# A three-layer kernel on one core: turns written out in line, memory weights on POOL, and a new table of marks for every engine

## The chip, the cores and the metric

The kernel runs on one core of a Trainium2 chip. The metric is device time in microseconds for one launch, as the median of several executions. The core has five instruction streams that run side by side, each in its own order: PE (TensorE, matrix products; the profile lists its weight loads apart, as PEld), DVE (VectorE), ACT (ScalarE), POOL (GpSimd) and SP (SyncE, which issues transfers). They meet only at semaphores.

## The reference, cut to what matters

The input x has 16 sequences of 512 rows and 256 columns. Each sequence goes through four blocks, all residual, each after a layer norm:

```python
x = x + attn_a(layernorm(x))   # 16 heads of 16, elu+1 features, 4 memories, causal sums
x = x + ffn(layernorm(x))      # 256 -> 1024 -> 256, ternary weights
x = x + attn_b(layernorm(x))   # 16 heads, rope, causal softmax over 512 keys
x = x + ffn(layernorm(x))      # the same ffn again
# in attn_a, per sequence and head (m is the memory):
rel = einsum('bhsd,mhd->mbhs', sq, memory_norms)
out_m = einsum('bhsd,mhde->mbhse', sq, memories) / clip(rel, EPS, None)[..., None]
weights = softmax(rel.mean(axis=-1), axis=0)          # over the 4 memories
mem_out = einsum('mbhse,mbh->bhse', out_m, weights)
out = g * mem_out + (1.0 - g) * local                 # g = sigmoid(gate)
```

Sequences don't depend on each other.

## The kernel before, in words

**Lanes and turns.** A sequence passes four lanes, one per block: lane 1 (attn_a, buffer xa), F1 (the first ffn, xf), lane 2 (attn_b, xb), F2 (the second ffn, xg). They form a pipeline over sequences. A turn is one step of it: while lane 2 works on sequence t, F2 finishes t-1 and F1 works on t+1; lane 1 ends t+1 and starts t+2. Its second part, `lane1_end`, comes first in a turn and `lane1_start` later. A filling part, one turn without F2 (t = 0), thirteen full turns, and an emptying part make up the run. The thirteen full turns (t = 1 to 13) are the body of a hardware loop, `with pe.Fori(1, B - 2) as it`, on each of the five engines; what is ahead of it and behind it is written out. In the body, semaphore targets such as `due(L, name, it, n)` are expressions of the loop's register; in what is written out they are constants.

**What sets the order.** Each engine's stream is merged from generators, one per lane, which yield a mark ahead of each piece of work; `in_order` always continues the generator with the lowest mark. The marks stand in the table `MARKS`, by lane, engine and kind of piece, with one number for each repetition. They order the instructions of an engine against each other and have no other effect. Kinds that matter here: lane 1 has T (norm), TT, PA (projections), V (values), SK, RM (mean of rel), ST (states), N and NC and NL (causal tiles), WO (output projection); lane 2 has T, PB, V, N (score tiles of head n for the row maxima), NM, NS (score tiles for the exponentials), PV, TP, OT, WO; an ffn lane has FT (norm), XB (adding b2), FTT, UP (eight blocks of the first product), DN (two blocks of the second).

```python
def in_order(*parts):
    heads = [next(part) for part in parts]
    while any(mark is not None for mark in heads):
        n = min((mark, n) for n, mark in enumerate(heads) if mark is not None)[1]
        heads[n] = next(parts[n], None)
```

**Who hands over to whom.** The turn's last DVE piece of F1 is the sum at L1084 that writes `xb`, twice in a turn; the norm of lane 2 in the next turn reads `xb` (L1035, the first DVE work of a turn). Lane 2 starts its scores (L1554 on PE) once the stacked q and k of half the heads have come back by DMA. L1270 is the row maximum on DVE, L898 the exponential on ACT. An UP block is four matmuls of 512 columns at L1402, DN are 64 matmuls at L1415 for an ffn; L650 on POOL takes the low part of each UP block, L644 adds b2 to the four row blocks of `xf` or `xg` in one POOL operation. In lane 1, L1185 makes the features and their row sums, L1192 (DVE) spreads the sums over 128 columns for a matmul, L1133 and L1136 form the exponents of the softmax over memories, L842 (ACT) takes the exponential, and `memory_weights_end` (L1142 to L1153) makes `winv`, the factor by which each memory's denominator is multiplied, on DVE. `combine` (L1107 on) is its first reader, in the first causal tile. L1094 (DVE), L804 (ACT) and L660 (POOL) mask and split the causal products; L693 (POOL) is the low part of the states. L1255 and L1259 on DVE are low parts of lane 2's q and k.

## Time and profile before

| what | value |
|---|---|
| device time, median of 3 runs | 2298.64 us (2289.67 to 2300.01) |
| device time of the profiled execution | 2286.95 us |
| its span, first to last instruction | 2285.2 us |
| mean granted TensorE clock | 0.937 of full |
| PE, PEld, DVE, ACT, POOL busy | 82%, 53%, 68%, 60%, 51% |
| DMA, mean over the span | 56 GB/s |

The profiled execution is 0.5% under the median of the three others. Busy shares are averages over a filling part, fourteen turns and an emptying part. A row of the view of windows gives a stretch, its length, each engine's busy time and instruction count in it, and the granted clock.

### The profile page before, as it was taken

The numbers are of one execution on the slowest core, as the hardware profiler recorded it, in microseconds if no ns is written. First come the engines' busy times: TensorE is split into PE (matmuls) and PEld (weight loads), VectorE is DVE, ScalarE is ACT, GpSimd is POOL, SyncE is SP. The second block draws the span as 40 slices with busy tenths as digits, with TensorE's granted clock in tenths as the row PEclk, the third lists the DMA queues.
The fourth block names the chain that finished last, engine by engine and source line by source line (L and its number), as shares of the span: only waits on it lengthen the run. The fifth ranks groups of instructions, "written<-read, shape, count | busy, mean of one in ns | idle before, by whom it ended". The sixth has DMA issues, their size and how long they took to land.

```text
span 2285.2 us, 52784 instructions
## 1 busy us (share of the span) xinstructions
PE 1875.6 (82%) x18306; PEld 1217.1 (53%) x18306; DVE 1555.1 (68%) x3707; ACT 1366.5 (60%) x2694; POOL 1174.0 (51%) x1168
## 2 busy tenths in 40 slices
PE   0446788989889797989899797989889798988886
PEld 0223455656556565656555565656555555655543
DVE  5645676867677676867677676867677686876351
ACT  0215376766667575666667575756667565666644
POOL 0235447364665547364655647365665736464322
PEclk9857899999999899999999999989999999999988
DMA  3101211213031211203021211203021210302020
GB/s 105 55 10 56 66 57 47 64 32 95 30 80 53 66 66 48 57 30 103 30 74 58 67 66 31 74 30 103 30 66 66 66 49 29 94 29 66 10 57 10
DMA packets 79287, 127.10 MB, mean 56 GB/s; under 512 B 13616, under 2 KB 65968, under 8 KB 74928
## 3 DMA queue, kind: packets, MB, share of 16 engines
q1 hardware_dynamic: 70576, 115.07, 18.0%
q10 hardware_dynamic: 8448, 8.39, 1.1%
q8 instruction: 181, 2.97, 0.5%
q14 instruction: 82, 0.67, 0.1%
HBM read 80.95 MB, written 42.47 MB: 54 GB/s over the span
## 4 chain that ended last, share of the span: by engine, by line
issue 38%; POOL 33%; PE 14%; DVE 8%; DMA 2%; ACT 2%; SPq 1%; POOLq 1%; DVEq 0%; ACTq 0%
POOL place L650 9%; POOL place L660 7%; POOL place L667 3%; POOL place L710 3%; POOL place L688 3%; POOL rstd L632 2%; PE bank L1415 2%; DVE mxs L1270 2%; PE bank L1402 1%; PE bank L1581 1%; POOL xf L644 1%; PE bank L1554 1%; PE bank L1366 1%; POOL place L713 1%; DMA qst<-by_dim 1%
## 5 line engine op out<-in xcount | busy, mean ns | idle before, releaser
L1270 DVE TENSOR_REDUCE mxs<-bank 128x1 f32<-128x128 f32 (+3 forms) x1024 | 429.8, 480 | 107.5 <-PE bank L1556 107.4
L898 ACT ACTIVATE place<-bank 128x512 f32<-128x512 f32 (+1 forms) x768 | 349.6, 527 | 148.1 <-PE bank L1570 146.7
L660 POOL TENSOR_TENSOR place<-am,place 128x512 f16<-128x512 f32 x256 | 291.4, 1160 | 162.0 <-ACT place L804 162.0
L650 POOL TENSOR_TENSOR place<-place 128x512 f16<-128x512 f32 x256 | 307.5, 1210 | 85.3 <-ACT place L792 84.5
L1554 PE MATMUL bank<-kst,qst 96*128 96x128 f16 (+3 forms) x1024 | 242.1, 308 | 31.4 <-DMA qst<-by_dim 23.0
L1568 PE MATMUL bank<-qst,kst 128*128 128x512 f16 (+3 forms) x1024 | 236.8, 304 | 22.7 <-DMA qst<-nmt 11.9
L1415 PE MATMUL bank<-w2q,place 128*128 128x256 f16 x2048 | 249.9, 273 | 3.2 <-POOL place L650 1.6
L1415 PEld LDWEIGHTS bank<-w2q,place 128*128 128x128 f16 x2048 | 195.2, 98 | 41.4 <-issue 7.9
L1556 PE MATMUL bank<-mask_qk,identb 128*128 128x128 bf16 x1024 | 217.1, 223 | 0.0
L1094 DVE SCALAR_TENSOR_TENSOR am<-bank,tri 128x512 f32<-128x512 f32 x256 | 166.2, 686 | 73.9 <-PE bank L1433 59.0
L629 POOL TENSOR_TENSOR ve<-mv,epsc 128x4 f32<-128x4 f32 x64 | 13.0, 203 | 382.7 <-DVE mv L1040 382.7
L804 ACT ACTIVATE place<-am 128x512 f16<-128x512 f32 x256 | 151.8, 627 | 90.2 <-DVE am L1094 90.2
L789 ACT ACTIVATE place<-bank,b1c 128x512 f32<-128x512 f32 x256 | 174.5, 682 | 44.2 <-PE bank L1402 21.4
L1570 PE MATMUL bank<-mask_kq,identb 128*128 128x128 bf16 x1024 | 186.0, 221 | 0.0
L1402 PE MATMUL bank<-xh,w1q 128*128 128x512 f16 x512 | 157.7, 390 | 27.7 <-ACT place L789 14.7
L792 ACT ACTIVATE place<-place 128x512 f16<-128x512 f32 x256 | 161.3, 630 | 8.1
L1568 PEld LDWEIGHTS bank<-qst,kst 128*128 128x128 f16 x1024 | 100.2, 98 | 114.0 <-DVE mxs L1270 33.0
L688 POOL TENSOR_TENSOR place<-place 128x512 f16<-128x512 f32 x64 | 80.9, 1275 | 154.3 <-ACT place L828 154.3
L1402 PE MATMUL bank<-xlo,w1q 128*128 128x512 f16 x512 | 157.9, 391 | 0.0
L1581 PE MATMUL bank<-place,vb 128*32 128x512 f32 (+3 forms) x2048 | 152.1, 438 | 5.4 <-DVE mxs L1270 3.4
L1554 PEld LDWEIGHTS bank<-kst,qst 96*128 96x128 f16 x1024 | 100.5, 100 | 91.0 <-DMA qst<-by_dim 31.1
L1356 PE MATMUL bank<-ident,place 128*128 128x128 f32 x512 | 85.6, 322 | 73.8 <-ACT place L755 73.8
(163 smaller groups left out, 4095.7 us busy)
## 6 DMA issues: line engine op xcount, KB each, us to landing
by_row<-place SPq DMA_DIRECT2D x128, 128.0 KB, 2.1
kst<-by_row SPq DMA_DIRECT2D x64, 256.0 KB, 3.3
qst<-by_row SPq DMA_DIRECT2D x32, 512.0 KB, 4.8
by_dim<-place SPq DMA_DIRECT2D x128, 128.0 KB, 3.1
kst<-by_dim SPq DMA_DIRECT2D x64, 256.0 KB, 3.9
qst<-by_dim SPq DMA_DIRECT2D x32, 512.0 KB, 6.2
xa<-x SPq DMA_DIRECT2D x16, 512.0 KB, 4.2
out<-xg ACTq DMA_DIRECT2D x16, 512.0 KB, 3.5
```

The costliest lines, as they stand in the source:

```text
L650: G.tensor_tensor(L.hl[:, m, :], L.hf[:, m % 2, :], L.hh[:, m, :], ALU.subtract).then_inc(s["hl"], 1)
L660: G.tensor_tensor(alp[:, n % 2, k, :], am[:, k, :], ahp[:, n % 2, k, :], ALU.subtract).then_inc(s["al"], 1)
L789: A.activation(L.hf[:, m % 2, :], bank_of(L, ("UP", m))[:, :], ACT.Relu, bias=b1c[:, m:m + 1]).then_inc(s["hf"], 1)
L898: A.activation(pf[h % SLOTS][:, S2_COL[k]:S2_COL[k] + S2_W[k]], bank_of(L2, ("S2", h, k))[:, 0:S2_W[k]], ACT.Exp, scale=D ** -0.5 / RS ** ...
L1270: V.tensor_reduce(mxs[:, g:g + 1], bank_of(L2, ("S1", n, k))[:, Q_AT[i]:Q_AT[i] + (i + 1) * P], AX, ALU.max).then_inc(s["mx"], 1)
L1402: ins = T.matmul(into[:, :], w1q[:, k, m * P:(m + 1) * P], a[:, k, :], start=(n == 0), stop=(n == 3))
L1415: ins = T.matmul(into[:, a * H:(a + 1) * H], part[:, m, cols], w2q[:, m, :], start=(m == 0 and part is L.hh), stop=(m == FT - 1 and part i ...
L1554: T.matmul(into[:, Q_AT[i]:Q_AT[i] + (i + 1) * P], L2.qst[0:STK, h, i * P:(i + 1) * P], L2.kst[0:STK, h, 0:(i + 1) * P], start=True, stop= ...
L1556: ins = T.matmul(into[:, Q_AT[i] + i * P:Q_AT[i] + (i + 1) * P], identb[:, :], mask_qk[:, :], start=False, stop=True, skip_group_check=True)
L1568: T.matmul(into[:, at:at + (NT - kt) * P], L2.kst[:, h, kt * P:(kt + 1) * P], L2.qst[:, h, kt * P:S], start=True, stop=True)
L1570: ins = T.matmul(into[:, at:at + P], identb[:, :], mask_kq[:, :], start=False, stop=True, skip_group_check=True)
L1581: ins = T.matmul(into[32 * j:32 * (j + 1), kt * P:S], vb[:, kt, h * VB:h * VB + 32], pf[h % SLOTS][:, KT_AT[kt]:KT_AT[kt] + (NT - kt) * P] ...
```

## The change

Five things change.

1. The hardware loops are gone: the thirteen full turns are a Python loop, so that each engine's stream holds all sixteen turns written out, with constants for semaphore targets and for the DMA addresses.
2. The memory weights. Before, DVE made the sum over memories (L1142), the product with the gate's factor (L1144), the reciprocal (L1148) and two products (L1153). Now DVE makes only the reciprocal of the exponentials, under a mark of its own (RE), and POOL makes two additions of pairs, a product with a gate factor made once at the start, and the two products (`memory_weights`, mark RW). DVE waits for POOL's result ahead of the first `combine`.
3. The spreading of the row sums (L1192) goes from DVE to ACT (mark SS).
4. L644 becomes two operations of half the size (XB 0 and 1), and DN's two sums wait for one each.
5. All marks are new.

```diff
-FFN = dict(up=8, hf=8, hh=8, hl=8, xb=1, dn=2, xffn=2)
+FFN = dict(up=8, hf=8, hh=8, hl=8, xb=2, dn=2, xffn=2)
...
 MARKS = {
...
         "dve": {
-            "N": [80, 85.8, 91, 98, 104.8, 110.6, 116.1, 1.7, 8, 19.1],
+            "N": [72.9, 77, 83, 90.4, 97.6, 103.4, 109.3, 1.7, 9.2, 13.3],
...
     3: {
...
         "pe": {
-            "FTT": [14.8],
-            "UP": [19.9, 21.1, 27, 28.7, 31.9, 35, 35.8, 37.5],
-            "DN": [37.6, 51.8],
+            "FTT": [7],
+            "UP": [13.7, 15.8, 16.7, 22.7, 24.9, 25.7, 27.9, 29.8],
+            "DN": [29.9, 37.2],
...
@@ on each of the five engines
-            with sp.Fori(1, B - 2) as it:
+            for it in range(1, B - 2):
                 in_order(after(lane1_end(it + 1), lane1_start(it + 2)), lane2(it), after(lane_f2(it - 1), lane_f1(it + 1)))
@@ POOL
-                yield mark("XB")
-                pool.wait_ge(s["xn"], due(L, "xn", t, NT))
-                G.tensor_tensor(X[:, :, :], X[:, :, :],
-                                b2bc[:, :].rearrange("p (a f) -> p a f", a=1).broadcast_to([P, NT, H]),
-                                ALU.add).then_inc(s["xb"], 1)
+                for j in range(2):
+                    yield mark("XB", j)
+                    if j == 0:
+                        pool.wait_ge(s["xn"], due(L, "xn", t, NT))
+                    two = slice(2 * j, 2 * j + 2)
+                    G.tensor_tensor(X[:, two, :], X[:, two, :],
+                                    b2bc[:, :].rearrange("p (a f) -> p a f", a=1).broadcast_to([P, 2, H]),
+                                    ALU.add).then_inc(s["xb"], 1)
...
+            def memory_weights(t):
+
+                s = s1
+                pool.wait_ge(s["rexp"], due(L1, "rexp", t, 1))
+                G.tensor_tensor(wpair[:, :, :, :], wexp[:, :, 0:M // 2, :], wexp[:, :, M // 2:M, :],
+                                ALU.add).then_inc(s["rpair"], 1)
+                pool.wait_ge(s["rpair"], due(L1, "rpair", t, 1))
+                G.tensor_tensor(wsum[:, :].rearrange("p (a h) -> p a h", a=KH), wpair[:, :, 0, :], wpair[:, :, 1, :],
+                                ALU.add).then_inc(s["rsum"], 1)
+                pool.wait_ge(s["rsum"], due(L1, "rsum", t, 1))
+                G.tensor_tensor(wgate[:, :], wsum[:, :], gates[:, 0, :], ALU.mult).then_inc(s["rgate"], 1)
+                pool.wait_ge(s["rgate"], due(L1, "rgate", t, 1))
+                pool.wait_ge(s["rrec"], due(L1, "rrec", t, 1))
+                for r in range(2):
+                    heads = slice(r * QH, (r + 1) * QH)
+                    G.tensor_tensor(winv[:, :, r, 0:M, :], wrec[:, :, :, heads],
+                                    wgate[:, :].rearrange("p (a m h) -> p a m h", a=KH, m=1)[:, :, :, heads]
+                                    .broadcast_to([P, KH, M, QH]), ALU.mult).then_inc(s["rcoef"], 1)
@@ ACT, lane1_start
+                yield at1("SS")
+                for half in range(KH):
+                    A.activation(ssb[:, half, :], onesf[:, :], ACT.Identity,
+                                 scale=ssum[:, half:half + 1]).then_inc(s["ssb"], 1)
@@ DVE
+            link(V.reciprocal(gates[:, 0, :], gates[:, 3, :]))
...
+                if n == 0:
+                    dve.wait_ge(s["rcoef"], due(L1, "rcoef", t, 2))
...
-            def memory_weights_end(t):
...
-                yield at1("PA", 4)
-                dve.wait_ge(s["sq"], due(L1, "sq", t, 4))
-                for half in range(KH):
-                    V.tensor_scalar(ssb[:, half, :], onesf[:, :], ssum[:, half:half + 1], None,
-                                    ALU.mult).then_inc(s["ssb"], 1)
...
-                memory_weights_end(t)
+                yield at1("RE")
+                dve.wait_ge(s["rexp"], due(L1, "rexp", t, 1))
+                V.reciprocal(wrec[:, :, :, :], wexp[:, :, :, :]).then_inc(s["rrec"], 1)
```

Two places where the new marks move work. The first is on PE, just ahead of lane 2's first score (head 0) in a full turn and at the row behind it. Before (L1402 is an UP block of F2, L1379 the projections of values and outputs, L1554 a score tile):

```order
L1379 MATMUL bank<-wh,xlo 128x256 x2
L1402 MATMUL bank<-xh,w1q 128x512 x2
L1402 MATMUL bank<-xlo,w1q 128x512 x2
...
L1402 MATMUL bank<-xh,w1q 128x512 x2
L1402 MATMUL bank<-xlo,w1q 128x512 x2
L1420 REGISTER_ALU
L1554 MATMUL bank<-kst,qst 128x128
```

The change (its lines are 13 further down: L1392 is L1379, L1415 is L1402, L1567 is L1554):

```order
L1392 MATMUL bank<-wh,xlo 128x256 x2
L1415 MATMUL bank<-xh,w1q 128x512 x2
L1415 MATMUL bank<-xlo,w1q 128x512 x2
L1415 MATMUL bank<-xh,w1q 128x512 x2
L1415 MATMUL bank<-xlo,w1q 128x512 x2
L1415 MATMUL bank<-xh,w1q 128x512 x2
L1415 MATMUL bank<-xlo,w1q 128x512 x2
L1567 MATMUL bank<-kst,qst 128x128
```

Before, four of F2's eight UP blocks stand ahead of the first score and four behind it; now seven stand ahead and one behind. In the table these are the marks UP of lane 3 under and over N 0 of lane 2 (30.9 before, 29 now).

The second place is DVE where lane 1 goes from its states to its first causal tile. Before (L1203 masks a state, L1142 to L1153 are the memory weights, L1047 is F1's low part, L1094 the causal mask):

```order
L1203 SCALAR_TENSOR_TENSOR place_1<-bank,bdmask 128x408
L1142 TENSOR_REDUCE wsum<-wexp 128x16
L1144 TENSOR_TENSOR wnum<-wexp,gates 128x64
L1147 ISA
L1148 RECIPROCAL wrec<-wnum 128x64
L1153 TENSOR_TENSOR winv<-wrec,wsum 128x2x16 x2
L1156 REGISTER_ALU
L1047 TENSOR_TENSOR xlo<-bank,xh 128x512 x2
L1091 REGISTER_ALU
L1094 SCALAR_TENSOR_TENSOR am<-bank,tri 128x512
```

The change (L1214 is L1203, L1283 is L1270, L1220 the reciprocal, L1127 is L1094, L1080 is L1047):

```order
L1214 SCALAR_TENSOR_TENSOR place_1<-bank,bdmask 128x408 x2
L1283 TENSOR_REDUCE mxs<-bank 128x1 x4
L1220 RECIPROCAL wrec<-wexp 128x64
L1127 SCALAR_TENSOR_TENSOR am<-bank,tri 128x512 x2
L1080 TENSOR_TENSOR xlo<-bank,xh 128x512 x2
```

Of the five operations one is left on DVE, and the causal mask now comes ahead of F1's low parts. On POOL, the additions and products stand between the low part of lane 1's last features and those of the states, and b2's two halves behind the first causal low parts:

```order
L714 TENSOR_TENSOR place_1<-place_1 128x512 x3
L691 TENSOR_TENSOR wpair<-wexp 128x32
L694 TENSOR_TENSOR wsum<-wpair 128x16
L697 TENSOR_TENSOR wgate<-wsum,gates 128x16
L702 TENSOR_TENSOR winv<-wrec,wgate 128x2x16 x2
L721 TENSOR_TENSOR bsl<-place_1 128x408 x2
L667 TENSOR_TENSOR place_1<-am,place_1 128x512 x2
L651 TENSOR_TENSOR xf<-xf,b2bc 128x512 x2
```

Before, L644 in one piece stood directly behind the second L693 (L721 now), ahead of the causal low parts.

## Rows read from the trace of the kernel before

**Rows 1.** The page: the span and the count of instructions.

```profile
span 2285.2 us, 52784 instructions
```

**Rows 2.** Windows: twelve turns by their first scores; thirteen by F1's last sums.

```profile
core 0: us, PE busy (x) PEld busy (x) DVE busy (x) ACT busy (x) POOL busy (x), PEclk, DMA share, GB/s
396.60:1949.70 1553.10, 1369.18 (x13728) 901.05 (x13728) 1131.60 (x2724) 1017.33 (x2019) 879.07 (x866) 0.96 0.21 59
366.07:2042.24 1676.17, 1481.76 (x14874) 975.20 (x14873) 1224.59 (x2951) 1101.35 (x2184) 951.67 (x936) 0.96 0.21 59
```

**Rows 3.** Windows from F1's last sum to the next first score, three of fifteen.

```profile
366.07:396.60 30.53, 22.04 (x180) 13.72 (x178) 20.76 (x49) 19.16 (x37) 23.05 (x23) 0.94 0.24 54
489.18:523.50 34.32, 21.99 (x181) 14.16 (x179) 21.12 (x49) 19.63 (x38) 23.41 (x24) 0.90 0.22 51
2042.24:2072.30 30.06, 21.94 (x180) 14.33 (x178) 20.78 (x49) 18.71 (x36) 22.57 (x23) 0.94 0.26 61
```

**Rows 4.** Windows from a turn's first score to F1's last sum, three of fifteen.

```profile
271.60:366.07 94.47, 85.39 (x886) 54.58 (x887) 71.15 (x176) 58.52 (x120) 43.02 (x43) 0.95 0.19 55
909.20:1007.21 98.01, 93.90 (x966) 61.88 (x967) 74.59 (x179) 65.11 (x132) 50.06 (x50) 0.97 0.20 60
1949.70:2042.24 92.54, 90.53 (x966) 60.43 (x967) 72.23 (x178) 64.86 (x131) 49.54 (x49) 1.00 0.21 63
```

**Rows 5.** PE's branch by line (ns min/median/max), and DVE's waits (total, times, longest us).

```profile
L1654 PEldq COMPARE_BRANCH  x13: 83/3329/3810, 487.5 to 2040.5; - x13
DVE stats L1035 <- issue: 32.9, 12, 2.9
```

**Rows 6.** Timeline at a turn's end, in the loop and written out.

```profile
1521.13 0.69 DVE L1084 TENSOR_TENSOR xb<-bank,xf 128x512 f32<-128x512 f32 x1 [1.77 <-PE bank L1415]
1524.72 0.43 DVE L1035 BATCH_NORM_STATS2 stats<-xb 128x6 f32<-128x256 f32 x1 [2.66 <-issue]
...
366.92 1.40 DVE L1035 BATCH_NORM_STATS2 stats<-xb 128x6 f32<-128x256 f32 x4
```

**Rows 7.** Timelines of DVE and POOL where the memory weights are made, two turns.

```profile
1218.26 3.00 DVE L1153 TENSOR_TENSOR winv<-wrec,wsum 128x32 f32<-128x32 f32 x2
1218.84 2.36 POOL L644 TENSOR_TENSOR xf<-xf,b2bc 128x1024 f32<-128x1024 f32 x1
...
1474.88 0.77 DVE L1153 TENSOR_TENSOR winv<-wrec,wsum 128x32 f32<-128x32 f32 x2
```

**Rows 8.** Instructions by line: durations in ns, min/median/max, and first and last start.

```profile
L1153 DVE TENSOR_TENSOR winv<-wrec,wsum x32: 179/670/2402, 100.2 to 1997.5; 128x32 f32<-128x32 f32 x32
L1142 DVE TENSOR_REDUCE wsum<-wexp x16: 252/254/255, 99.1 to 1995.8; 128x16 f32<-128x64 f32 x16
L1144 DVE TENSOR_TENSOR wnum<-wexp,gates x16: 214/215/248, 99.2 to 1996.0; 128x64 f32<-128x64 f32 x16
L1192 DVE TENSOR_SCALAR am<-onesf,ssum x32: 255/280/1191, 89.9 to 1982.3; 128x128 f32<-128x128 f32 x32
L629 POOL TENSOR_TENSOR ve<-mv,epsc x64: 198/203/206, 72.7 to 2254.7; 128x4 f32<-128x4 f32 x64
```

**Rows 9.** Timelines: an UP block on PE; the memory weights' exponential and first reader.

```profile
1042.33 0.59 PE L1402 MATMUL bank<-xh,w1q 128*128 128x512 f16 x2
1042.76 0.59 PE L1402 MATMUL bank<-xlo,w1q 128*128 128x512 f16 x2
1043.19 0.22 PE L1554 MATMUL bank<-kst,qst 96*128 96x128 f16 x1
...
1471.90 0.27 ACT L842 ACTIVATE wexp<-wdif 128x64 f32<-128x64 f32 x1
1484.93 0.38 DVE L1107 SCALAR_TENSOR_TENSOR den<-bank,winv 128x24 f32<-128x24 f32 x2 [0.73 <-PE bank L1466]
```

**Rows 10.** The page's instruction queue, and the longest issue wait in 271.6 to 366.07.

```profile
q8 instruction: 181, 2.97, 0.5%
PEld bank L1581 <- issue: 4.1, 17, 0.3
```

174 lines of the change are left out of this document (81 added, 93 removed), and 39 rows, old and new, of the table MARKS.

## The prediction

> **What bounds the kernel now.** I read the page first, then the stretches of a turn as windows, then the chain of single instructions where one turn goes over into the next. The page gives the span, 2285.2 us [rows 1]. The profiled execution took 2286.95 us, 0.5% under the median of the other three runs (2298.64); the sum below is made against its span, and the last step scales by 2298.64 / 2286.95 = 1.0051.
>
> The run is a row of turns. Twelve of them, from first score to first score, take 1553.10 us, 129.4 each; all thirteen full turns take 1676.17 us, 128.9 each, 73% of the span [rows 2]. What one turn gains counts about thirteen times, so the turn is what has to be read. It falls into two stretches. From F1's last sum to lane 2's first score (call it the **opening**) there are about 34 us in which PE is busy for 22 [rows 3]. From the first score to F1's last sum (the **body**) there are 92.5 to 98 us in which PE is busy for 90.5 of 92.5, 98%, DVE for 78% and ACT for 70% (the undisturbed one of rows 4). So the body is PE's, or waits of a fraction of a microsecond between PE and the others, and the opening is latency: lane 2's norm, projections, rope and the transfer of q and k, one behind the other, with F2's beginning beside them.
>
> **Part 1, the loop.** In the loop DVE's last sum of a turn starts at 1521.13 and the first statistics of the next at 1524.72, 3.6 us on, with an idle time that nothing in the profile ends. In the turn that is written out (t = 0) the same two start at 366.07 and 366.92 [rows 6], 0.85 us apart. The waits say it in one row: 32.9 us in 12 waits ahead of this operation [rows 5]; the loop jumps back twelve times. On PE the branch itself lasts 3.3 us in the median and 3.8 at most [rows 5]. This idle time lies on the path, since the norm that waits is the head of lane 2's chain. Its price is at least 32.9 us. The whole opening shows more: the twelve behind a jump take 33.7 to 36.2 us, 34.7 in the mean (the first is in rows 3), the two reached without a jump 30.5 and 30.1 [rows 3]. The rest of the difference goes with the granted clock, 0.90 behind a jump and 0.94 without [rows 3]: PE is idle longer there, and runs longer at its lower level of 1.2 GHz. I take the openings' difference, 34.7 - 30.3 = 4.4, times 12: **53 us**, with 33 as the lower end.
>
> The Trainium skill, page "Advanced Engine Details and Errata", section "Control Flow Timing", gives about 108 ns for a compare-and-branch. By that price alone, an estimate, twelve jumps would be worth 1.3 us and this part nothing. The trace disagrees on PE, 3.3 us against 0.11.
>
> What else is written in line costs nothing that I can see: the register operations go away, but the body of the written-out turn t = 0 took 94.5 us [rows 4], no less than those in the loop although F2 has no part in it. I count 0 for them.
>
> **Part 2, the collision.** The second of the two products at L1153 takes 0.18 us or 2.40 us [rows 8]. Both turns in rows 7 show why: it starts within 0.03 us of POOL's 2.4 us operation on b2, and in five of twelve turns DVE stands until POOL is done (the pair 3.00 us instead of 0.77). The bodies of these five turns take 95.2 to 98.0 us, 96.5 in the mean, the other eight in the loop 93.4 (one of each in rows 4). The change takes these products off DVE and halves the POOL operation. 5 x 3.1 = **15 us**; the lower end is the products' own 5 x 2.2 = 11.
>
> **Part 3, work moved off DVE.** L1142, L1144 and L1153 are 0.25 + 0.21 + 0.77 = 1.2 us a turn, in a run in which DVE has no idle time and behind which lane 1's causal mask waits; L1192 is 2 x 0.28 [rows 7, 8]. Against it, a chain of five tiny POOL operations: their price isn't in the trace; the nearest is 0.20 us for 128x4 [rows 8], so some 1.0 to 1.6 us with their handovers. From the exponential at 1471.90 to the first reader of winv at 1484.93 there are 13 us [rows 9], which hides them, and ACT's two operations of about 0.3 us lie in a body where ACT is idle for 28 us [rows 4]. If that cover were gone they would cost their 1.6 us a turn, 21 us in all.
>
> **Part 4, the order.** Three UP blocks of F2 go from the body to the opening. One is 0.86 us of PE (1042.33 to 1043.19 [rows 9]), so 2.6 us leave a stretch in which PE is full and enter one in which it is idle for 12 of 34 us. With part 3 that makes 3.8 us of body. The marks bound it from above. They are an order and no times; but before, lane 2's N 0 and F1's DN 1 on PE and DVE are 91.9 apart (30.9 to 122.8), and the trace has 92.5 at the least and 93.4 in the mean for an undisturbed body. The new ones are 86.9 apart (29.0 to 115.9), 5.0 less. Between 0 (the order brings nothing, other waits fill in) and 5.0 I take 4.5 for the body, nearer to the upper end, since 3.8 of it have rows of their own. For the opening the mark of N 0 comes 1.9 earlier although PE has more to do there; between 0 and 1.9 I take 1.0. Together 5.5 x 13 = **71 us**, with 0 and 90 as ends. Part 5, b2 in halves, has no term of its own: the addition starts about 1475.5 (behind the products of rows 7), and F1's last sum, which reads it, at 1521.1 [rows 6].
>
> **Outside the full turns** (609 us) there are no jumps. The turns t = 0 and t = 14 get most of the order's gain, 5 and 4 us, the two ends, where a lane has the engines nearly alone, 4: **13 us**, ends 0 and 20.
>
> **The sum.** 53 + 15 + 71 + 13 = 152 us. 2285.2 - 152 = 2133, or 2135 us of device time on the profiled execution, times 1.0051: **2144 us**. A full turn would be 128.9 - 152 x (139 / 152) / 13 = 118.2 us.
>
> **The rivals.**
>
> *The jump's time isn't repaid* (0.15). Only the 33 us of idle time come back, the opening keeps its low clock since PE has as little to do there, and a collision of DVE and POOL comes up elsewhere. For it: POOL gets more operations, and the written-out openings that I compare with are only two. Against it: F2's UP blocks now fill the opening. 20 + 15 us less: 2179 us.
>
> *The order brings nothing* (0.10). The lanes' chains, not PE, set the body; what leaves it makes room for waits. For it: DVE and ACT are idle for a quarter of the body and PE's "busy" includes the tails of its matmuls. Then 53 + 15 = 68 us: (2286.95 - 68) x 1.0051 = 2230 us.
>
> *The order brings more* (0.07): the values of lane 1 now come earlier behind its projections, both lanes shorten, and the clock holds. 3 us a turn more: 2105 us.
>
> *Slower* (0.04): the engines wait for their instructions. Written out, every turn is new code. The profile has 181 loads of 2.97 MB on the instruction queue, 16 KB each [rows 10], some 11 a turn. If each stopped its engine as the jump stops PE, 3.3 us, a turn would take 36 us longer and the kernel about 2610 us. It decides from 152 / 3.3 = 46 uncovered loads on, between three and four a turn. Against it: in the body of the written-out turn PE's longest wait for issue is 0.3 us [rows 10], with its share of loads. The Trainium skill, same page, section "ISA Cache", gives lines of 16 KB and few of them, which is why a jump far back must load anew and why a straight run could miss too; the size of the loads agrees, the stops don't show.
>
> *The change doesn't do what it says*: it does, in the order of each engine, so there is no chance for it.
>
> **How the numbers follow.** The forecast has 0.64, the rivals 0.15, 0.10, 0.07 and 0.04. The predicted time is the forecast's. The range of 2105 to 2220 us takes in the first rival and the ends of the order's term short of nothing; outside stay the second rival, the slow one and part of the third, together under 0.2. A measurement of this kernel tells about 0.5% from no change. Faster by more: all cases but the slow one and a hundredth of the second rival in which POOL's new chain costs its uncovered price as well, 0.95; within 0.5%: 0.01; slower by more: 0.04.
>
> **What would show it.** Right: DVE's first statistics start 0.85 us behind F1's last sum in every turn; openings of 29 to 30 us at a clock of 0.94 or more; bodies of about 89 us with PE still over 95% busy and seven UP blocks ahead of the first score; no operation of DVE near 2.4 us in the body; b2's additions about 1.2 us each; turns of 118 us whose bodies differ by less than before (they spread from 92.5 to 98). Wrong: waits of DVE for `rcoef` ahead of the first `combine`; issue waits of over 1 us in the written-out turns; openings over 32 us; bodies of 92 us or more, which would strike part 4; a turn whose length swings by 3 us, which would say that the collision only moved.

## The result, and the profile after

| what | before | after |
|---|---|---|
| device time, median (4 runs each) | 2299.32 us (2289.67 to 2309.44) | 2195.57 us (2189.11 to 2200.08) |
| ratio, 95% interval | | 0.9546 (0.9496 to 0.9596) |
| profiled execution, its span | 2286.95, 2285.2 us | 2200.08, 2198.2 us |
| mean granted clock | 0.937 | 0.942 |
| thirteen turns, from the first score of t = 1 to that of t = 14 | 1675.7 us | 1596.0 us |
| opening, body, mean of t = 1 to 13 | 34.4, 94.6 us | 31.6, 91.05 us |

The change makes the kernel 4.5% faster, inside the range and of the forecast sign, but it brings 104 us where 155 were forecast; between the spans 87 where the sum had 152. The two differences are 17 us apart because the profiled execution of the kernel before is faster than its other four, and that of the kernel after the slowest of its four. So a step that is read from one pair of profiles, as all of those below are, can be several us off.

**Turns.** The view of windows of the kernel after: thirteen turns, an opening, the body of t = 7 and the body of t = 9, and the first 3 us behind the first score in t = 7 and t = 9 (columns as in [rows 2]; the last three are granted clock, DMA share, GB/s). t = 7 kept its clock at the scores, t = 9 didn't:

```profile
391.21:1987.20 1595.99, 1489.98 (x14873) 978.58 (x14873) 1178.06 (x2873) 1104.56 (x2212) 965.39 (x1029) 0.97 0.22 62
1217.51:1248.77 31.26, 25.11 (x191) 15.33 (x190) 20.47 (x49) 23.09 (x43) 25.71 (x27) 0.95 0.23 52
1128.15:1217.51 89.36, 87.68 (x955) 59.41 (x955) 70.16 (x173) 61.20 (x127) 47.86 (x53) 1.00 0.22 66
1371.44:1462.97 91.53, 89.42 (x955) 60.06 (x955) 70.17 (x172) 61.72 (x127) 48.39 (x53) 0.98 0.21 64
1128.15:1131.15 3.00, 3.00 (x26) 2.07 (x27) 2.27 (x6) 2.54 (x5) 2.42 (x3) 1.00 0.91 318
1371.44:1374.44 3.00, 3.00 (x13) 1.50 (x14) 1.69 (x4) 1.95 (x3) 2.64 (x3) 0.56 0.91 315
```

A turn is 122.8 us where 118.2 were forecast. The body of t = 7 is the one that was forecast ("about 89"), that of t = 9 is 2.2 us longer with the same count of matmuls. The last two rows show where most of that begins: in the first 3 us of scores PE does 26 matmuls in the one and 13 in the other, at a granted clock of 1.00 and 0.56. How late head 4's score tile ("tile 4") starts behind head 0's shows this for every turn: 7.51 us in t = 1 and t = 7, and 8.8 to 10.4 us in the other eleven, in which the clock is low at the first scores.

**The end of a turn.** The timeline of DVE, to be read against [rows 6]:

```profile
1462.97 0.69 DVE L1117 TENSOR_TENSOR xb<-bank,xf 128x512 f32<-128x512 f32 x1 [1.25 <-PE bank L1428]
1463.58 0.28 DVE L1160 TENSOR_TENSOR xlo<-bank,xh 128x128 f16<-128x128 f32 x1
1463.78 0.74 DVE L1068 BATCH_NORM_STATS2 stats<-xb 128x6 f32<-128x256 f32 x2
```

The statistics start 0.81 us behind the last sum, here and in all thirteen turns; no wait for issue is left ahead of them. The 32.9 us of [rows 5] are gone.

**The weights and b2.** Groups by line, with the mean of one in ns behind the busy time, against [rows 7, 8]:

```profile
L651 POOL TENSOR_TENSOR xf<-xf,b2bc 128x512 f32<-128x512 f32 x32 | 40.0, 1273 | 8.0 <-ACT place L783 8.0
L702 POOL TENSOR_TENSOR winv<-wrec,wgate 128x32 f32<-128x32 f32 x32 | 7.1, 242 | 50.4 <-DVE wrec L1220 50.4
L691 POOL TENSOR_TENSOR wpair<-wexp 128x32 f32<-128x32 f32 x16 | 4.0, 251 | 180.2 <-ACT wexp L874 180.2
L697 POOL TENSOR_TENSOR wgate<-wsum,gates 128x16 f32<-128x16 f32 x16 | 3.5, 221 | 1.3
```

POOL's chain is 0.25 + 0.22 + 0.22 + 2 x 0.24 = 1.2 us, and no wait of DVE for its result shows. No product lasts 2.4 us any more, and in the bodies DVE has no operation of that length.

**Ahead of the first score.** PE in t = 9, from the end of UP block 5 on:

```profile
1367.51 0.60 PE L1415 MATMUL bank<-xlo,w1q 128*128 128x512 f16 x2
1370.24 0.61 PE L1415 MATMUL bank<-xh,w1q 128*128 128x512 f16 x2 [2.13 <-ACT place L817]
1370.68 0.59 PE L1415 MATMUL bank<-xlo,w1q 128*128 128x512 f16 x2
1371.44 0.23 PE L1567 MATMUL bank<-kst,qst 96*128 96x128 f16 x1 [0.16 <-DMA qst<-by_dim]
```

The UP blocks moved ahead are there, but the last of them (block 6) stands 2.13 us for a bank that ACT has to read first. ACT is late because it waited 0.71 us for POOL's rope and then copied values for 1.06. The granted clock falls to its lower level, 1.2 GHz, at 1371.8, stays there for 3.4 us, and the scores pay. In the two turns without it PE was idle for as long (2.14 us), about 0.5 us earlier against the score than in most others; the experiments below don't bear out that this place decides. In the kernel before, PE was idle for 3.0 to 3.9 us of the last nine, in three pieces of which none was longer than 1.72, and the clock fell at the score in three turns of thirteen.

**The opening** is 31.6 us in the mean where 29.3 were forecast. ACT's timeline in the written-out opening of the kernel before (F1's last sum at 366.07), and of one after (1462.97):

```profile
370.51 2.08 ACT L755 ACTIVATE place<-xb,shift,rstd 128x256 f32<-128x256 f32 x4 [3.83 <-POOL shift L635]
372.49 1.13 ACT L804 ACTIVATE place<-am 128x512 f16<-128x512 f32 x2
373.53 1.05 ACT L762 ACTIVATE xh<-bank 128x512 f16<-128x512 f32 x2
374.49 0.26 ACT L809 ACTIVATE xh<-bank 128x128 f16<-128x128 f32 x1
374.64 2.07 ACT L755 ACTIVATE place<-xg,shift,rstd 128x256 f32<-128x256 f32 x4
377.83 1.21 ACT L869 ACTIVATE place<-bank 64x512 f32<-64x512 f32 x2 [1.11 <-PE bank L1366]
```

```profile
1467.37 2.08 ACT L783 ACTIVATE place<-xb,shift,rstd 128x256 f32<-128x256 f32 x4
1470.32 2.07 ACT L783 ACTIVATE place<-xg,shift,rstd 128x256 f32<-128x256 f32 x4 [0.87 <-POOL shift L639]
1472.30 0.25 ACT L837 ACTIVATE xh<-bank 128x128 f16<-128x128 f32 x1
1472.45 2.03 ACT L790 ACTIVATE xh<-bank 128x512 f16<-128x512 f32 x4
1475.92 1.21 ACT L901 ACTIVATE place<-bank 64x512 f32<-64x512 f32 x2 [1.43 <-PE bank L1379]
```

The new marks put F2's normalisation (`xg`) ahead of the copies of lane 2's transposed rows (`xh`). These start 9.5 us behind the last sum, not 7.5, and the first projection (the `place<-bank` row) is copied at +12.95, not +11.76: 1.2 us later on lane 2's chain.

### The profile page after: what moved, and what is told of

Its sections match the earlier page's. It is cut to its first block, busy times and chain, and to the rows that moved or that the text cites. A ratio compares the mean times of both kernels' runs of the same rounds, so it can differ in the third digit from the quotient of the medians.

```text
span 2198.2 us, 47411 instructions
## 1 busy us (share of the span) xinstructions
PE 1885.9 (86%) x18306; PEld 1220.8 (56%) x18306; DVE 1500.7 (68%) x3612; ACT 1369.6 (62%) x2726; POOL 1190.9 (54%) x1280
## 3 DMA queue, kind: packets, MB, share of 16 engines
q8 instruction: 147, 2.41, 0.5%
## 4 chain that ended last, share of the span: by engine, by line
PE 50%; DVE 18%; ACT 11%; POOL 8%; DMA 7%; issue 3%; SPq 2%; POOLq 0%; ACTq 0%; DVEq 0%
PE bank L1428 10%; PE bank L1594 6%; PE bank L1567 5%; PE bank L1581 5%; PE bank L1415 4%; DMA qst<-by_dim 4%; DVE mxs L1283 3%; DVE place L1201 3%; ACT place L930 2%; POOL place L741 2%; POOL place L738 2%; PE bank L1392 2%; DVE stats L1068 2%; PE bank L1463 2%; PE bank L1569 2%
## 5 line engine op out<-in xcount | busy, mean ns | idle before, releaser
L1283 DVE TENSOR_REDUCE mxs<-bank 128x1 f32<-128x128 f32 (+3 forms) x1024 | 433.4, 482 | 120.5 <-PE bank L1569 118.9
L657 POOL TENSOR_TENSOR place<-place 128x512 f16<-128x512 f32 x256 | 301.6, 1186 | 66.4 <-ACT place L820 64.4
L1567 PE MATMUL bank<-kst,qst 96*128 96x128 f16 (+3 forms) x1024 | 252.3, 314 | 34.2 <-DMA qst<-by_dim 11.7
L1428 PE MATMUL bank<-w2q,place 128*128 128x256 f16 x2048 | 255.7, 275 | 1.8 <-POOL place L657 1.6
L1581 PE MATMUL bank<-qst,kst 128*128 128x512 f16 (+3 forms) x1024 | 232.6, 302 | 14.6 <-DVE mxs L1283 7.5
L1569 PE MATMUL bank<-mask_qk,identb 128*128 128x128 bf16 x1024 | 222.3, 226 | 0.0
L1127 DVE SCALAR_TENSOR_TENSOR am<-bank,tri 128x512 f32<-128x512 f32 x256 | 166.8, 684 | 52.5 <-PE bank L1446 41.7
L1415 PE MATMUL bank<-xh,w1q 128*128 128x512 f16 x512 | 161.8, 399 | 38.7 <-ACT place L817 36.0
L714 POOL TENSOR_TENSOR place<-place 128x512 f16<-128x512 f32 x64 | 80.8, 1272 | 187.7 <-ACT place L856 169.7
L1369 PE MATMUL bank<-ident,place 128*128 128x128 f32 x512 | 98.5, 341 | 79.1 <-ACT place L783 77.8
L1415 PE MATMUL bank<-xlo,w1q 128*128 128x512 f16 x512 | 161.1, 398 | 0.0
L1567 PEld LDWEIGHTS bank<-kst,qst 96*128 96x128 f16 x1024 | 102.8, 102 | 103.4 <-ACT place L930 40.4
```

What stands on the lines that cost most here:

```text
L657: G.tensor_tensor(L.hl[:, m, :], L.hf[:, m % 2, :], L.hh[:, m, :], ALU.subtract).then_inc(s["hl"], 1)
L1283: V.tensor_reduce(mxs[:, g:g + 1], bank_of(L2, ("S1", n, k))[:, Q_AT[i]:Q_AT[i] + (i + 1) * P], AX, ALU.max).then_inc(s["mx"], 1)
L1415: ins = T.matmul(into[:, :], w1q[:, k, m * P:(m + 1) * P], a[:, k, :], start=(n == 0), stop=(n == 3))
L1428: ins = T.matmul(into[:, a * H:(a + 1) * H], part[:, m, cols], w2q[:, m, :], start=(m == 0 and part is L.hh), stop=(m == FT - 1 and part i ...
L1567: T.matmul(into[:, Q_AT[i]:Q_AT[i] + (i + 1) * P], L2.qst[0:STK, h, i * P:(i + 1) * P], L2.kst[0:STK, h, 0:(i + 1) * P], start=True, stop= ...
L1569: ins = T.matmul(into[:, Q_AT[i] + i * P:Q_AT[i] + (i + 1) * P], identb[:, :], mask_qk[:, :], start=False, stop=True, skip_group_check=True)
```

## The experiments

Each row has the ratio to the kernel before on the same chip; the medians of different rows can come from different chips. The last three columns come from the first scores and F1's last sums in the timeline of the profiled execution, as in the table above.

| run | median, us | ratio (95%) | span | 13 turns | opening | body |
|---|---|---|---|---|---|---|
| before, written out | 2245.04 | 0.980 (0.9757 to 0.9843) | 2236.9 | 1630.5 | 31.4 | 94.0 |
| change, in the loop | 2223.02 | 0.9691 (0.965 to 0.9731) | 2220.6 | 1621.3 | 34.5 | 90.2 |
| change, old marks | 2221.77 | 0.9701 (0.966 to 0.9742) | 2218.8 | 1608.5 | 31.3 | 92.7 |
| filler at the score | 2199.86 | 0.9599 (0.9561 to 0.9637) | 2193.0 | 1596.6 | 33.3 | 89.5 |
| filler in the idle stretch | 2173.51 | 0.9472 (0.9437 to 0.9508) | 2170.7 | 1576.4 | 31.6 | 89.7 |
| F2's norm later | 2197.49 | 0.9575 (0.9538 to 0.9611) | 2198.7 | 1599.3 | 33.2 | 89.8 |
| both of these | 2195.18 | 0.9567 (0.9531 to 0.9604) | 2190.8 | 1596.3 | 33.2 | 89.6 |
| weights back on DVE | 2202.54 | 0.9595 (0.9559 to 0.9631) | 2202.1 | 1600.6 | 31.8 | 91.4 |
| before written out, b2 in halves | 2241.66 | 0.9766 (0.9718 to 0.9814) | 2241.6 | 1630.6 | 31.7 | 93.9 |
| change, b2 in one piece | 2191.90 | 0.9552 (0.9506 to 0.9599) | 2187.9 | 1587.7 | 31.5 | 90.6 |
| change, again | 2193.75 | 0.956 (0.9524 to 0.9597) | 2191.9 | 1593.9 | 31.8 | 90.9 |
| filler of five | 2177.71 | 0.9491 (0.9455 to 0.9527) | 2175.1 | 1580.0 | 31.7 | 89.8 |

### One part alone: the kernel before, written out

```diff
@@ on each of the five engines
-            with sp.Fori(1, B - 2) as it:
+            for it in range(1, B - 2):
```

> The kernel before with the thirteen full turns written out in line and nothing else changed: part 1 alone. Theory A (the forecast's term): DVE's first statistics come 0.85 us behind F1's last sum in every turn, openings 30 to 31 us instead of 34.7, and 53 us less in all, ratio 0.977. Theory B (only the idle time of the jump comes back, the clock's part stays): openings about 32 us, 33 us less, ratio 0.986. In both the collisions at L1153 stay, 0.18 or 2.40 us, and bodies of 92.5 to 98 us.

2245.04 us, 50 less by the medians, 48.3 by the spans. The openings lose 2.95 us each in the mean, 3.2 in the twelve behind a jump; the statistics start 0.84 us behind the last sum everywhere. An opening (t = 10), a body without and one with the collision, and the collision itself, from the windows and the timelines of DVE and POOL:

```profile
1491.67:1522.67 31.00, 23.40 (x181) 14.21 (x179) 20.68 (x49) 18.62 (x36) 22.45 (x23) 0.89 0.22 52
1023.56:1115.88 92.32, 90.38 (x966) 60.58 (x967) 72.29 (x179) 65.50 (x132) 50.32 (x50) 1.00 0.21 64
1522.67:1617.54 94.87, 90.54 (x966) 60.46 (x967) 74.52 (x179) 65.72 (x133) 50.60 (x50) 1.00 0.22 63
```

```profile
1570.00 3.00 DVE L1153 TENSOR_TENSOR winv<-wrec,wsum 128x32 f32<-128x32 f32 x2
1569.66 0.96 POOL L693 TENSOR_TENSOR bsl<-place 128x408 f16<-128x408 f32 x1 [0.73 <-ACT place L846]
1570.58 2.36 POOL L644 TENSOR_TENSOR xf<-xf,b2bc 128x1024 f32<-128x1024 f32 x1
```

Three things follow. The jump's 2.7 us are repaid at a clock of 0.89 as well. Most of the clock's share that the prediction added is not: only three of the thirteen openings reach the 0.94 or 0.95 of the two without a jump in [rows 3], and they take 30.8 us in the mean, near to those two with 30.3; the other ten stay at 0.89 or 0.84 and take 31.6. And the collision comes in seven turns now, not five. Each costs 2.2 us: those seven bodies are 94.8 in the mean, the four free of it and of a low clock at the score 92.6.

### The jump in the new order

```diff
@@ the changed kernel, on each of the five engines
-            for it in range(1, B - 2):
+            with sp.Fori(1, B - 2) as it:
```

> The changed kernel with the hardware loop put back on all five engines: part 1 taken away alone. If the jump costs in the new order what it cost in the old one (2.8 us of idle time in each of 12 turns at the least, 4.4 by the openings), the kernel loses 33 to 53 us: ratio to the kernel before 0.969 to 0.978 instead of 0.955. If the new order needs the written-out turns (its opening is waited for by both lanes), it loses more than 53 us, ratio over 0.978.

2223.02 us, 27 more than the changed kernel; 22.4 by the spans, 33 by the ratios to the kernel before on the two chips. DVE's waits have the row of [rows 5] again:

```profile
DVE stats L1068 <- issue: 33.3, 12, 2.9
```

The openings are 34.5 us, 2.8 more. The bodies are 90.2, 0.8 less than in the changed kernel, because the clock falls at the first score in eight turns of thirteen here and in eleven there. So what the loop takes away in the opening is partly given back: the size of part 1 depends on where PE stands idle, and in this order it is 22 to 33 us.

### The order: the changed kernel with the old marks

```diff
@@ MARKS, all lanes and engines, as before; where there was none:
+            "RW": [76.5],
+            "SS": [59.4],
+            "RE": [77.3],
@@ F1; F2's are [25.6, 25.7]
+            "XB": [79.3, 79.4],
```

> Everything of the change but the order: turns written out, weights on POOL, row sums by ACT, b2 in halves, with the marks of before (the new pieces get marks at the old places). Theory A: the jump's 53 us and the collisions' 15 us come back, no operation of DVE near 2.4 us in the body and bodies of 92.5 to 94 us, ratio 0.970; the order is then worth 0.970 - 0.955 = 1.5%, 35 us, half of the forecast's 71. Theory B: the memory weights on POOL cost something in the old order (POOL's b2 addition meets another operation of DVE, or the causal low parts come later), ratio 0.975 to 0.98, and the order is worth more than 1.5%.

2221.77 us. From the kernel before, written out, to this one are 18.1 us of span, 22.1 in the thirteen turns: what the moved weights, the halved b2 and the row sums on ACT bring in the old order. From this one to the changed kernel are 20.6 us of span, of which 12.5 lie in the thirteen turns: **all that the order brought**, where 71 - 16 = 55 and 13 outside had been forecast. Its bodies are 92.7 us, only 1.6 more than the changed kernel's, and its openings 0.4 less in the mean of t = 1 to 13 (0.6 less in those of t = 2 to 14, which lie between the first scores). With the second profile of the changed kernel (below) the thirteen turns give 14.6, and the medians 26 to 28 us with the ends, of 55 + 13 forecast: the amount is uncertain by some us, the shortfall isn't.

The openings of the old order are short or long by the granted clock. Two of them, t = 10 and t = 12, as windows, with lane 2's first two projection matmuls on PE and the copy of the finished projection on ACT:

```profile
1482.69:1512.85 30.16, 21.88 (x180) 14.01 (x178) 19.67 (x49) 18.28 (x36) 22.69 (x24) 0.94 0.24 58
1492.90 0.61 PE L1379 MATMUL bank<-xh,wh 128*128 128x512 f16 x2 [0.39 <-DVE xlo L1080]
1494.41 1.21 ACT L901 ACTIVATE place<-bank 64x512 f32<-64x512 f32 x2 [1.12 <-PE bank L1379]
1727.82:1760.61 32.79, 24.34 (x179) 14.65 (x177) 20.18 (x49) 19.28 (x38) 23.66 (x24) 0.84 0.25 59
1738.09 1.04 PE L1379 MATMUL bank<-xh,wh 128*128 128x512 f16 x2
1740.87 1.21 ACT L901 ACTIVATE place<-bank 64x512 f32<-64x512 f32 x2 [2.44 <-PE bank L1379]
```

In t = 12 the clock is low from 4.8 to 15.0 us behind F1's last sum, the projection's matmuls run under it, and the copy starts at +13.05 instead of +11.7. So it is in seven of the thirteen turns (+12.7 to +13.05, clock 0.89 or less); in the other six (0.94 or 0.95) it starts at +11.7 and the openings take 30.4 us in the mean. The changed kernel's at that clock take 31.4: the 1.2 us at the head of the chain. But its projections begin at +11.4 and not +10.2, in most turns when the low stretch is over, and it loses less to the clock there.

### The clock at the first score, paid for in the opening

```diff
@@ scores, on PE; FILL = 8
+                if h == 0:
+                    into = take(L2, ("S1", 0, 0), t)
+                    for n in range(FILL):
+                        T.matmul(into[:, :], identh[:, :], w1q[:, 0, 0:4 * P], start=True, stop=True)
```

> The changed kernel with eight more matmuls of 512 columns on PE (1.7 us in all) just ahead of lane 2's first wait for its stacked q and k, into the bank that the first score overwrites; their results are not used. In the changed kernel PE stands idle for some 2.5 us just ahead of the first score, and in eleven of thirteen full turns the clock is at its lower level for 3.4 or 6.8 us from about the first score on. Theory A (this idle time lets the clock fall, and the fall costs the body 1.65 us a turn): with the added work the clock stays up at the first score in most turns, score of head 4 starts 7.5 us behind that of head 0 instead of 9.2, and the kernel gains 10 to 20 us in all. Theory B (the fall has another cause): the same stretches at half clock, and no gain or a loss of up to 1.7 us a turn, 22 us.

2199.86 us, no gain. But the clock stays up: score tile 4 comes 7.50 us behind tile 0 in every turn, and the bodies are 89.5, as in windows of t = 9:

```profile
1369.63:1458.98 89.35, 87.67 (x956) 59.40 (x954) 70.04 (x173) 60.46 (x126) 47.08 (x52) 1.00 0.21 62
```

The fillers stand directly on the path, and the opening pays 1.7 us for the 1.5 that the body wins. (In t = 7, 10 and 13 the clock falls 4 us ahead of the score instead, and these openings take 34.5 us where most take 32.8.) The 1.5 us are the clock's, and what PE does just ahead of the scores decides them.

### The same fillers inside the idle stretch

```diff
@@ ffn, on PE, ahead of the UP block
+                    if m == 6 and L is F2 and t < B - 1:
+                        into = take(L2, ("S1", 0, 0), t + 1)
+                        for n in range(FILL):
+                            T.matmul(into[:, :], identh[:, :], w1q[:, 0, 0:4 * P], start=True, stop=True)
```

> The changed kernel, with the same eight matmuls of 512 columns into a bank that nobody reads yet as in the run before, but issued by PE ahead of F2's UP block 6, where PE now stands idle for 2.13 us in most turns, and not behind it. If the clock falls at the first score because of that idle stretch, and if the idle stretch can take the matmuls without delaying the first score: score h4 starts 7.5 us behind score h0 in all full turns, bodies 89.4 us instead of 91.05, openings unchanged at 31.4; 1.65 us x 11 turns = 18 us of span less than the changed kernel (2180), a ratio of 0.947 to 0.950 to the kernel before. Rival: the matmuls last longer than the gap, and what the body gains the opening gives back as in the run before: bodies 89.4, openings 32.8 or more, span 2193 to 2200. Second rival: the idle stretch moves to another place ahead of the first score, h4 stays at 9 us and nothing changes.

2173.51 us: **faster than the changed kernel by 22 us, 1%**. Nobody reads what the fillers write; the first score begins its bank anew. PE's timeline ahead of the first score of t = 10, and the first 3 us of scores, the body and the opening of t = 9 in windows:

```profile
1476.31 0.59 PE L1420 MATMUL bank<-xlo,w1q 128*128 128x512 f16 x2
1476.74 1.89 PE L1417 MATMUL bank<-w1q,identh 128*128 128x512 f16 x8
1479.04 0.60 PE L1420 MATMUL bank<-xh,w1q 128*128 128x512 f16 x2 [0.41 <-ACT place L818]
1479.48 0.59 PE L1420 MATMUL bank<-xlo,w1q 128*128 128x512 f16 x2
1480.08 0.23 PE L1572 MATMUL bank<-kst,qst 96*128 96x128 f16 x1
```

```profile
1359.52:1362.52 3.00, 3.00 (x26) 2.06 (x27) 2.27 (x6) 2.85 (x5) 2.64 (x3) 1.00 0.90 309
1359.52:1448.86 89.34, 87.67 (x955) 59.44 (x955) 69.99 (x173) 61.62 (x127) 48.38 (x53) 1.00 0.22 66
1328.10:1359.52 31.42, 27.28 (x200) 16.62 (x198) 20.63 (x49) 23.23 (x44) 25.86 (x27) 0.89 0.25 54
```

Eight matmuls take 1.9 of the 2.13 us, a wait of 0.41 us is left, and block 6 starts no later. Tile 4 comes at 7.5 to 7.7 us in all thirteen turns. The openings stay at 31.6. In this order the clock matters little in them: the seven at 0.95 take 31.5 us in the mean, the six at 0.89 31.7. In the scores the same low stretch costs 1.65. Of the 27.5 us between the spans 19.6 lie in the thirteen turns; 18 had been expected.

### F2's normalisation behind lane 2's copies

```diff
@@ MARKS, lane 3
         "act": {
-            "FT": [6.3],
-            "FTT": [9.4],
+            "FT": [8.5],
+            "FTT": [12.1],
@@ its FTT on DVE and on PE
-            "FTT": [12],
+            "FTT": [13.6],
-            "FTT": [7],
+            "FTT": [10.6],
```

> The changed kernel with four marks moved: F2's normalisation stands behind lane 2's transposed copies on ACT (before: ahead of them, four operations of 0.58 us), and its transposes on PE and DVE are later accordingly. Theory: these four operations are what put lane 2's first projection 1.2 us later on ACT in each turn; openings go from 31.5 to about 30.3, bodies stay at 91; 1.2 us x 13 = 16 us of span less (2182), a ratio near 0.948. Rival: F2's UP blocks come later by the same amount, PE is idle longer ahead of the first score, and the wait for ACT's hidden half of UP block 4 or 5 takes the place of the one removed: openings 31.5 or more, no gain (span 2198 or more).

A miss: 2197.49 us, no gain. Bodies are 89.8, since block 6 waits only 1.0 to 1.1 us now; the piece right ahead of the score is at most 1.6 us in twelve turns, and 2.7 in t = 6, the one turn in which the clock falls there. But the openings are 33.2, not 30.3. ACT's timeline of t = 9 (F1's last sum at 1343.89):

```profile
1351.79 0.28 ACT L837 ACTIVATE xh<-bank 128x128 f16<-128x128 f32 x1 [1.42 <-PE bank L1490]
1351.96 1.08 ACT L790 ACTIVATE xh<-bank 128x512 f16<-128x512 f32 x2
1352.92 2.07 ACT L783 ACTIVATE place<-xg,shift,rstd 128x256 f32<-128x256 f32 x4
1356.33 1.21 ACT L901 ACTIVATE place<-bank 64x512 f32<-64x512 f32 x2 [1.35 <-PE bank L1379]
1357.57 1.08 ACT L790 ACTIVATE xh<-bank 128x512 f16<-128x512 f32 x2
```

The copies do start 1.4 us earlier, at +8.1, and the first projection at +12.4 instead of +12.95. That is one of eight turns whose openings have a clock of 0.90 or less (33.9 us in the mean); in the other five, at 0.95, the projection is copied at +11.4 to +11.5, the whole gain, and the openings take 32.1. So the projections meet the low clock again, as with the old marks, and this is one part of the loss. Then F2's own transposes and copies stand between lane 2's projections: the second projection is copied 2.5 us behind the first and not 1.6, the third 7.8 and not 4.9. So what was taken off the head of the chain came back in its middle as well, and there in every turn. So the 1.2 us at the head are real as a row, but not as a saving in this place.

### Both

```diff
@@ MARKS as in the last run, and ahead of the UP block
+            "FT": [8.5],
+            "FTT": [12.1],
...
+                        for n in range(FILL):
+                            T.matmul(into[:, :], identh[:, :], w1q[:, 0, 0:4 * P], start=True, stop=True)
```

> Both of the two edits ahead in one kernel: the eight matmuls ahead of UP block 6, and F2's normalisation behind lane 2's transposed copies. If both theories hold and their gains are apart: bodies 89.4, openings 30.3, turns 119.7 instead of 122.7, 18 + 16 = 34 us of span less than the changed kernel (2164), a ratio near 0.940. If F2 being later leaves less room ahead of the first score, the matmuls delay it: openings 31.5 to 33 and bodies 89.4, no more than the better one of the two alone.

2195.18 us: the clock is held already (bodies 89.6), and the opening of 33.2 stays. Here the fillers bring nothing, as they should where there is no low clock to remove.

### The weights back on DVE, in the new order

```diff
@@ POOL
-                yield at1("RW")
-                memory_weights(t)
@@ DVE, lane1_start, under the mark RE
-                V.reciprocal(wrec[:, :, :, :], wexp[:, :, :, :]).then_inc(s["rrec"], 1)
+                memory_weights_end(t)
```

> The changed kernel, written out and in the new order, but the memory weights' sum, product, reciprocal and the two products are all back on DVE, at the mark where the change has the reciprocal; b2 stays in halves. If the move off DVE is worth what the sum gave it: DVE has 1.2 us more a turn in a run without idle time, and the second product meets POOL's addition in some turns, now for 1.2 us at most since that addition is halved. 1.2 us x 13 = 16 us, and up to 5 x 1 us: span 2214 to 2220, ratio 0.963 to 0.966. Rival: DVE's 1.2 us are covered by waits elsewhere in the body: span 2198 to 2203, ratio 0.955 to 0.958, bodies 91.0 as in the changed kernel.

2202.54 us, 7 to 9 more than the changed kernel's two medians. The span is in the rival's range, the ratio just over it: a difference at the edge of what can be told, and about half of the 16 us of the first theory. Its products show why it is less than in the old order, by the group of that line:

```profile
L1164 DVE TENSOR_TENSOR winv<-wrec,wsum 128x32 f32<-128x32 f32 x32 | 5.6, 215 | 1.7
```

In the full turns they take 0.19 and 0.18 us. In the kernel before the first took 0.67 in every turn [rows 8, the median], because it met POOL's L693, and the second 2.40 in some. The new marks put both POOL operations elsewhere, so on DVE the work is 0.25 + 0.21 + 0.37 = 0.8 us a turn and not 1.2.

### b2 in halves alone

```diff
@@ the kernel before, written out; DN's sums wait for one half each
-FFN = dict(up=8, hf=8, hh=8, hl=8, xb=1, dn=2, xffn=2)
+FFN = dict(up=8, hf=8, hh=8, hl=8, xb=2, dn=2, xffn=2)
@@ POOL
-                yield mark("XB")
+                for j in range(2):
+                    yield mark("XB", j)
```

> The kernel before, written out (the run that put turns in line and nothing else: span 2236.9, ratio 0.980, seven turns with a second product of 2.40 us), with b2 added in two pieces of half the size, one behind the other; the memory weights stay on DVE. Theory of part 2: DVE's product stands until POOL's operation is done, so half the operation is half the stand: the second product lasts 1.3 us at most, the seven turns win 1.1 to 3 us each, 10 to 18 us of span (2220 to 2227), ratio 0.973 to 0.976. Rival: it meets the second piece as well and stays at 2.4 us (no gain, 0.980); or the halving alone shifts the collision away, then as much as the kernel of the old order has (2219, 0.970), and moving the weights brings nothing there.

2241.66 us, 3 less than without the halves, and within what can be told from no change; the 10 to 18 us expected did not come. The collision is halved, as expected:

```profile
1446.52 1.92 DVE L1156 TENSOR_TENSOR winv<-wrec,wsum 128x32 f32<-128x32 f32 x2
1446.18 0.96 POOL L696 TENSOR_TENSOR bsl<-place 128x408 f16<-128x408 f32 x1 [0.72 <-ACT place L849]
1447.10 2.51 POOL L647 TENSOR_TENSOR xf<-xf,b2bc 128x512 f32<-128x512 f32 x2
```

The pair takes 1.92 us instead of 3.00; the second product lasts 1.3 us in six of the thirteen turns. DVE stands some 9 us less in these turns, and the thirteen turns take the same 1630.6. At the scores this run loses more than the one without the halves: the clock is low there in three turns (two without), and in seven others tile 4 starts at 8.2 to 8.6 us at full clock (7.9 to 8.1 in the eleven others without). Ahead of the scores ACT stands 0.9 us for POOL's low part of an UP block here, 0.35 to 0.5 without the halves, but it does so also in turns that lose nothing; what costs the 9 us stays open. The halves also end a second collision that the prediction didn't have: in the kernel before (14 turns) and in the one written out (13) F2's addition makes one of DVE's L1255 last 2.1 us instead of 0.7 or 0.8, in the opening, and none lasts over 1.6 here. The openings are no shorter for it (31.7 against 31.4).

So in the old order it is the work moved off DVE that brings the gain: from here to the changed kernel with the old marks are 20 us by the medians, 22 in the thirteen turns. The weights' 1.2 us a turn, the 0.5 of collision left and the row sums' 0.56 went together, and no run parts them.

### b2 in one piece, in the changed kernel

```diff
-                for j in range(2):
-                    yield mark("XB", j)
+                yield mark("XB")
@@ MARKS, lane 3 and lane 4
-            "XB": [9.4, 10.6],
+            "XB": [9.4],
-            "XB": [77.8, 79.1],
+            "XB": [77.8],
```

> The changed kernel with b2 added in one piece of 2.4 us as before (at the mark of the first half), all else as changed. The weights' products are on POOL here, so there is nothing on DVE for it to meet in the old place. Theory: halving has no part of its own, within 0.3% of the changed kernel (0.952 to 0.957, span 2195 to 2203). Rival: another operation of DVE with two inputs from SBUF now meets it and lasts 2.2 us or more, or lane 1's subtractions on POOL come 1.2 us later and the body with them: ratio 0.960 or more, span 2210 or more.

2191.90 us, beside 2193.75 for the changed kernel on the same chip. Halving b2 brings nothing by itself in the new order.

### The changed kernel again, and five fillers

```diff
-FILL = 8
+FILL = 5
```

> The changed kernel itself, unaltered, on the same chip as the run behind it, so that the two can be compared directly: 2190 to 2200 us, a ratio of 0.955.

> The changed kernel with five instead of eight matmuls of 512 columns ahead of UP block 6 (1.2 us instead of 1.9 of the 2.13 us that PE stands idle there; nobody reads their result). If less than the whole gap has to be filled: h4 7.5 us behind h0 in all turns and a ratio of 0.947 as with eight, or a little less, since eight ran 0.4 us up to the wait's end with little to spare. Rival: the clock falls again in part of the turns (h4 at 9): 0.948 to 0.955, bodies between 89.6 and 91. In either case faster than the kernel of the run ahead.

Six runs of each on the same chip: 2193.75 us (2190.27 to 2198.03) and 2177.71 us (2173.71 to 2181.74), which don't overlap. Five fillers, 1.2 us of the stretch, bring 16 us; the clock falls in one full turn (t = 5, tile 4 at 9.17 us), as the rival had it. Eight have the lowest ratio, 0.9472, but the intervals overlap (0.9437 to 0.9508, 0.9455 to 0.9527), so the two aren't told apart.

The second profile of the unaltered kernel has the low clock at the scores in ten turns of thirteen, not eleven, and in other ones: t = 2, 9 and 13 are free of it. The idle piece is 2.1 us long in these three too, and begins 3.0 to 3.4 us ahead of the score, later than in most of the ten.

## Why the prediction had the sign right and the time 52 us too low

By the parts, in the thirteen turns unless said otherwise:

| step of the prediction | forecast | shown by | measured |
|---|---|---|---|
| part 1, the jump | 53 | before to before written out | 45.2 (span 48.3) |
| part 2, the collision | 15 | before written out to old marks | 22.1 with part 3 |
| part 3, off DVE, inside part 4 | 16 | the same | in the row above |
| part 4, the order, without part 3 | 55 | old marks to changed kernel | 12.5 |
| outside the full turns | 13 | before to after | 7.3 |
| sum | 152 | spans | 87 |

The measured rows add up: 45.2 + 22.1 + 12.5 + 7.3 = 87.1. The forecast's last step has a slip of 2 us: 2135 x 1.0051 is 2146, not 2144; 2144 is the span's 2133 scaled, and the rivals at 2179 and 2105 carry it too. "Five of twelve turns" in part 2 are five of thirteen.

**Part 1 held, with a mechanism half right.** The idle time behind the jump is gone in every turn, at the price of [rows 5]. The step from 33 to 53 us was an addition for the clock, read from two openings as a base of 30.3 us. Both had the clock at 0.94; of the thirteen that were freed or written out ten don't reach it, and the twelve behind a former jump are 31.4, so 3.2 us each and 39 in all. The other 6 or 7 us came in the bodies (94.0 for 94.6), to which I gave nothing. In the new order the jump is worth 22 to 33 us.

**Parts 2 and 3 were near**: 22 for 31. The mechanism stands, and shows that the engines meet at more than semaphores. A DVE product that begins while one of these POOL operations runs ends just behind it: in the run written out the first product ends at 1570.67, 0.05 us behind L693, and the second at 1573.00, 0.06 us behind L644. The Trainium skill, page "SBUF — State Buffer", section "Who interferes with whom", has this as an exclusive lock that goes to whichever starts first; these rows and the 1.92 us with a halved operation agree. What I had not seen is that the first product's 0.67 us is a collision as well, in every turn. The price of one was too high (3.1; 2.2 shown), their number isn't fixed by the program (5 turns, then 7), and how much the moved work gave outside the collisions isn't shown alone: 22 us came with the weights, the row sums and the halves together, and in the new order the weights are worth 7 to 9 us.

**Part 4 is the step that failed.** It took 5.5 us a turn, of them 4.5 in the body and 1.0 in the opening, and of the 4.2 that are left without part 3 the runs found 1.0. Three things are in the difference.

- *The clock at the first score.* "2.6 us leave a stretch in which PE is full and enter one in which it is idle" is what happened, but the blocks moved don't fill that stretch evenly: they run ahead until their bank is missing and leave PE idle in one piece, right ahead of the densest work. With the clock held the thirteen turns are 19.6 us shorter, so the order is worth up to 32 of the 55, and its bodies 89.7, near the forecast's 89. Up to, since the old order was not run with fillers: its clock is low at the scores in two turns, t = 1 and 7, an estimate of 4 us from their tile 4 (10.7 and 9.6 us, 8.2 in the mean of the others).
- *The opening.* 29.3 was 34.4 less the jump and less 1.0 for the order. It is 31.6: 1.1 from the base above, 1.0 that didn't come, 0.2 more. The mark of N 0 had moved by 1.9; marks are an order, and the chain (F2's norm on ACT ahead of lane 2's copies) got longer at its head by 1.2 us. Moving it back lost more in the middle and to the clock.
- *The ends.* 7 us instead of 13.

By device time the result, 2195.57 us, lies between the first rival ("the jump's time isn't repaid", 35 us off the sum, 2179 us) and the second ("the order brings nothing", 2230). Neither was the mechanism alone: the jump was repaid, though with the openings' clock still low in the run that had part 1 alone, as the first rival said, and the order brought something, which the clock took back in part. The signs named beforehand told it: openings of 31.6 (under the 32 that would have struck it, over the 29 to 30 that would have confirmed it), and bodies of 91 (89 forecast, 92 the limit). Two signs of being wrong did appear, with another cause than the one they were named for. Turns swing from 120.6 to 124.4 us, and not by a collision: the clock at the scores makes most of the difference between the shortest (t = 7) and its neighbours. And PE's weight loads wait for issue over 1 us once a turn, 1.4 at most; in the loop they reached 2.3, and the loads on the instruction queue fell from 181 [rows 10] to 147, so the engines didn't wait more for their instructions than before.

**What stays open** is which idle piece makes the clock fall. In the changed kernel one piece of 2.1 us did so in eleven turns, in its second profile in ten, and in the loop (2.05 us) in eight. The turns spared in the first profile are two in which it began early (3.9 us ahead of the score), those spared in the second are three in which it began late (3.0 to 3.4), so its place against the score doesn't decide alone. In the kernel before, 3.0 to 3.9 us in three pieces did so in three turns. Filling the piece, or cutting it to 1.1 us, mostly holds the clock; why a given turn keeps it isn't shown.

## What to carry to other kernels

When work of PE is moved from a dense stretch into an idle one, look at what idle time is left right ahead of the dense stretch, and price the low clock there in the row of the dense one: here 1.5 us a turn, over half of what the order would have brought (up to 2.5 with the clock held, 1.0 without). A handful of matmuls that nobody reads, placed inside a wait that must be waited anyway, bought it back; the same ones a step further on the path bought nothing. And base a term on what a stretch is in the mean, not on the two samples that happen to be free of the thing removed: these two had a higher clock than most of those they stood for.
